# Values five tiles behind keys, the first maxima between the last value chunks, the last value group rounded on ScalarE

## The chip, the cores and the metric

One core of a Trainium2 chip runs the program; the other cores are idle. A time is device microseconds of one execution. TensorE (PE) multiplies matrices into PSUM, VectorE (DVE) and GpSimd (POOL) do element work and reductions, ScalarE (ACT) does activations and copies, SyncE (SP) issues most of the DMAs in the order in which they are written. Every engine works its own list in order and waits on semaphores.

## The reference

```python
x = x + tanh(g_xattn[0]) * xattn(layernorm(x), ctx_2048, Wq, bq, Wkv, bkv, Wp, bp)
x = x + tanh(g_ffn[0]) * moe(layernorm(x), Wg, W1, W3, W2, Ws1, Ws3, Ws2)
# xattn: 800 queries (8 x 100), 2888 keys (8 x 361), 16 heads of 32
q, k = fq_sym(q * scale, axis=-1), fq_sym(k, axis=-1)  # 8 bits, one step for a row and head
v = fq_sym(v, axis=2)                                  # one step for a column, over all 2888 keys
attn = fq_unsigned(softmax(q @ k.T))                   # 8 bits, one step for a row
out = (attn @ v) @ Wp + bp
```

The rounding of a value column needs the largest value over all keys: a value group must be complete before any of it is rounded. The mixture of experts behind the attention is not touched.

## The kernel before

Tokens stand in 7 tiles of 128 (the last has 32), keys in 23 tiles of 128, values in 4 groups of 128 columns (4 heads each), each group in 6 chunks of up to 512 keys: five of 512 and one of 328, 24 chunks in all.

**Projection loop.** For each key tile TensorE makes the key product (`project`, L549) and, from tile LEAD on, one value chunk (`make_values`, L575, line L586), both in fp32. A key tile goes through VectorE (read L1053, amplitude, rounding, multiplying back L1119), ScalarE (first of three bf16 parts, L911), GpSimd (rest, L1470), ScalarE (second part, L916) and GpSimd (third part, L1474), and SyncE stores it in DRAM (`key_parts`, L446). A product may start when VectorE has read the last but one; a value chunk when ScalarE has copied the last but one out of PSUM (`copy_values`, L899). VectorE bounds each copied chunk (`bound_values`, L1076) and after the sixth rounds the group to int16 and casts it to bf16 (`quantise_values`, L1083 to L1093); SyncE then transposes it (`transpose_values`, L438). With LEAD = 3, twenty chunks are in the loop and four behind it.

**Hand-over.** When all key tiles are stored and the last product is done, SyncE loads head 0's keys by four DMA transposes (`load_keys`, L427); head 1's follow when all value chunks are done, because their place overlays the context.

**Attention.** There are 100 tiles in a written order: for each of 16 heads six query tiles, and for each group of four heads one tile that holds the last 32 queries of the four. For each tile TensorE makes the scores twice, in four pieces for the maxima (`for_max`; VectorE reduces them, L1166) and in three for the exponentials (`for_exp`; ScalarE, L936, to 8-bit integers). VectorE turns the maxima into the bias of the exponentials (L1186). SyncE transposes the tile's probabilities (`transpose_p`, L472; two buffers), GpSimd widens them to bf16 (L1495), and TensorE multiplies them by the values (`weigh_values`, L645) four steps later. TensorE's order mixes these (`attention_step`, L657). SyncE's list interleaves the probabilities' transposes with key loads for later heads and, ahead of the second tile's probabilities, the transpose of the last value group. Four zero fills (L1135, L1137) on VectorE precede attention, and the last group's `quantise_values` stands in VectorE's list behind the second tile's maxima.

## Time and profile before

| | before |
|---|---|
| median of 3 runs | 1048.98 us (1046.87 to 1051.36) |
| profiled execution | 1048.64 us, of which the span is 1047.1 us |
| busy in the span | PE 94%, DVE 60%, ACT 49%, POOL 43% |
| chain that ended last, by engine | PE 52%, POOL 15%, DVE 11%, ACT 9%, issue 7%, DMA 5% |

The span runs from the first to the last instruction of the trace; the execution's own time lies 1.5 us above it. A row gives the start of an instruction, or of a run of like ones (x8), its length and what it does, and in brackets the time for which its engine had been idle and what released it. The projections of the keys and values lie between 50 and 208 us, attention between 208 and 597 us, the output projection and the mixture of experts behind.

### The profile page before, as it was taken

What the parts mean: (1) busy time and instruction counts of PE and PEld (TensorE: products, weight loads), DVE (VectorE), ACT (ScalarE), POOL (GpSimd) and SP (SyncE); (2) the same over time, 40 slices, a digit from 0 to 9 for tenths busy, and PEclk for the clock granted to TensorE, in tenths of its full rate; (3) what the DMA queues carried; (4) which work ended last, traced back from release to release, by engine and by line L of the source; (5) the groups of instructions that cost most, each with busy time, mean ns of one, the idle gap of its engine ahead of it and who ended that gap; (6) DMA issues with size and microseconds to landing.
All of it is one profiled execution on the core that took longest, in us unless ns stands there. A gap on an engine that the chain in (4) does not pass through costs nothing.

```text
span 1047.1 us, 16611 instructions
## 1 busy us (share of the span) xinstructions
PE 983.5 (94%) x5718; PEld 498.6 (48%) x5719; DVE 627.8 (60%) x1120; ACT 509.9 (49%) x1058; POOL 450.4 (43%) x319
## 2 busy tenths in 40 slices
PE   6999999879999999999999899999999999999993
PEld 3444444324334444444444457555656665666551
DVE  5686675499989999999999665811111111111156
ACT  2432223259999999999999822111211222121110
POOL 2053333227977777777677820371111111111165
PEclk9999999979999999999999998999999999999997
DMA  9974654678888888888776644144544654643155
GB/s 334 207 260 192 210 190 189 179 159 142 136 134 133 141 143 130 138 143 148 131 139 103 104 171 171 71 180 146 194 182 162 233 192 184 239 171 129 50 168 156
DMA packets 268272, 172.45 MB, mean 165 GB/s; under 512 B 239344, under 2 KB 239344, under 8 KB 265904
## 3 DMA queue, kind: packets, MB, share of 16 engines
q1 hardware_dynamic: 258512, 140.14, 54.7%
q0 software_dynamic: 9696, 31.47, 8.8%
q8 instruction: 39, 0.64, 0.3%
q14 instruction: 25, 0.20, 0.1%
HBM read 68.67 MB, written 44.63 MB: 108 GB/s over the span
## 4 chain that ended last, share of the span: by engine, by line
PE 52%; POOL 15%; DVE 11%; ACT 9%; issue 7%; DMA 5%; POOLq 0%; SPq 0%; DVEq 0%; ACTq 0%
PE ps L751 17%; POOL arena_a L1495 10%; PE ps L771 9%; ACT arena_a L936 7%; PE ps L603 6%; PE ps L586 6%; PE ps L563 6%; DVE span_max L1166 5%; POOL expert_in L1513 2%; PE ps L645 2%; PE ps L688 2%; DMA q_t<-parts 2%; PE ps L781 1%; PE ps L762 1%; POOL arena_b L1552 1%
## 5 line engine op out<-in xcount | busy, mean ns | idle before, releaser
L1166 DVE TENSOR_REDUCE span_max<-ps 128x1 f32<-128x481 f32 (+2 forms) x400 | 351.3, 904 | 21.0 <-PE ps L603 12.8
L936 ACT ACTIVATE arena_a<-ps,exp_bias,q_step 128x962 uint8<-128x962 f32 (+1 forms) x288 | 330.2, 1157 | 23.7 <-DVE exp_bias L1186 12.5
L1495 POOL CAST arena_a<-arena_a 128x3072 bf16<-128x3072 uint8 x100 | 274.3, 2752 | 123.3 <-DMA arena_a<-arena_a 113.8
L603 PE MATMUL ps<-arena_a,q_t 128*128 128x481 bf16 (+1 forms) x864 | 226.2, 376 | 20.0 <-DVE span_max L1166 8.0
L751 PE MATMUL ps<-arena_a,xt 128*128 x544 | 172.2, 459 | 1.8 <-issue 1.8
L1327 DVE TENSOR_TENSOR proj_d<-ps,proj_f 128x352 f32<-128x352 f32 x48 | 25.1, 524 | 200.5 <-ACT proj_f L984 200.5
L990 ACT COPY proj_r<-ps 128x128 f32<-128x128 f32 x144 | 28.4, 270 | 224.2 <-PE ps L762 224.2
L603 PEld LDWEIGHTS ps<-arena_a,q_t 128*128 128x128 bf16 x864 | 62.8, 98 | 150.9 <-ACT arena_a L936 69.5
L771 PE MATMUL ps<-arena_a,proj_r 128*128 (+3 forms) x288 | 133.5, 600 | 0.7 <-ACT proj_r L990 0.7
L751 PEld LDWEIGHTS ps<-arena_a,xt 128*128 128x128 f32 x544 | 100.4, 190 | 61.2 <-issue 17.9
L645 PEld LDWEIGHTS ps<-v_q,arena_a 128*128 128x128 bf16 x2400 | 75.5, 96 | 28.1 <-POOL arena_a L1495 9.8
L586 PE MATMUL ps<-arena_a 128*128 128x512 f32 (+1 forms) x192 | 83.0, 578 | 4.5 <-ACT xt L899 3.6
L563 PE MATMUL ps<-arena_a 128*128 128x512 f32 x184 | 82.6, 593 | 1.4 <-DVE proj_f L1053 1.1
L1519 POOL DMA_DIRECT2D xt<-expert_in x36 | 19.4, 539 | 147.8 <-PE ps L781 145.8
L645 PE MATMUL ps<-v_q,arena_a 128*128 128x32 bf16 (+1 forms) x2400 | 78.5, 178 | 2.8 <-POOL arena_a L1495 1.5
L603 PE MATMUL ps<-arena_b,q_t 128*128 128x481 bf16 (+1 forms) x288 | 75.0, 369 | 4.0 <-ACT arena_a L936 0.3
L771 PEld LDWEIGHTS ps<-arena_a,proj_r 128*128 128x128 f32 (+1 forms) x288 | 52.6, 192 | 50.4 <-issue 46.7
L751 PE MATMUL ps<-arena_a,q_t 128*128 128x352 f32 x224 | 73.2, 472 | 0.0
L1345 DVE COPY xt<-ps 128x512 f32<-128x512 f32 x34 | 23.5, 692 | 68.9 <-PE ps L771 68.9
L1523 POOL DMA_DIRECT2D expert_out<-xt x34 | 18.5, 544 | 106.5 <-DVE xt L1345 106.5
L984 ACT ACTIVATE proj_f<-ps 128x352 f32<-128x352 f32 x48 | 22.3, 464 | 83.5 <-PE ps L751 83.5
L586 PEld LDWEIGHTS ps<-arena_a 128*128 128x128 f32 x192 | 36.7, 193 | 49.2 <-issue 41.1
(167 smaller groups left out, 917.7 us busy)
## 6 DMA issues: line engine op xcount, KB each, us to landing
arena_a<-in_w_up SPq DMA_DIRECT2D x18, 1408.0 KB, 6.4
arena_a<-in_w_down SPq DMA_DIRECT2D x18, 768.0 KB, 8.4
key_parts<-parts SPq DMA_DIRECT2D x23, 512.0 KB, 2.7
expert_in<-xt SPq DMA_DIRECT2D x42, 256.0 KB, 3.0
xt<-expert_in POOLq DMA_DIRECT2D x36, 256.0 KB, 3.0
expert_out<-xt POOLq DMA_DIRECT2D x34, 256.0 KB, 2.3
arena_a<-in_ctx_t SPq DMA_DIRECT2D x3, 1536.0 KB, 13.2
expert_out<-xt SPq DMA_DIRECT2D x17, 256.0 KB, 3.1
```

The costliest lines, as they stand in the source:

```text
L563: last = mm(ps[:, 2 + j % 2, :], src, w_qkv[:, 0 if j < T else 1, k, :], start=(k == 0), stop=(k == DC - 1))
L586: last = mm(ps[:, 4 + v % 2, 0:w], w_qkv[:, 2, k, g * P:(g + 1) * P], ctx_sb[:, k, c * BANK:c * BANK + w], start=(k == 0), stop=(k == DC - 1))
L603: last = mm(ps[:, bank + b, 0:w], q_t[:, head, t * P:(t + 1) * P], k_t[head % NK][:, a:a + w], start=True, stop=True)
L645: last = mm(ps[:, OUT_BANK, 0:w], p_t[n % NPT][:, c, :], v_q[:, c, a:a + w], start=(c == 0), stop=(c == 2 * PC - 1))
L751: last = mm(ps[:, 1 + 2 * q + w, 0:INTER], src(k), arena_a[:, bass.ds(col + (w * DC + k) * INTER, INTER)], start=(k == 0), stop=(k == DC - 1))
L771: last = mm(ps[:, 6 + q, :], h_t[0:IW[c], q, c * P:(c + 1) * P], arena_a[0:IW[c], bass.ds(col + UPC + c * D, D)], start=(c == 0), stop=(c ...
L936: nc.scalar.activation(halves[:, :, a:a + w], ps[:, bank:bank + 2, 0:w], ACT.Exp, bias=exp_bias[:, n % 2:n % 2 + 1], scale=step_of, accum_ ...
L990: last = nc.scalar.copy(h_t[0:IW[c], q, c * P:(c + 1) * P], ps[0:IW[c], 5, c * P:(c + 1) * P])
L1166: v.tensor_reduce(span_max[:, n % 2, j:j + 1], ps[:, bank:bank + len(blocks), 0:w], AX.XY, ALU.max).then_inc(s_max, 1)
L1327: v.tensor_tensor(h_mul[:, q, 0:INTER], ps[:, 2 + 2 * q, 0:INTER], h_act[:, q, 0:INTER], ALU.mult).then_inc(s_hm, 1)
L1345: v.tensor_copy(y_rows[:, q, :], ps[:, 6 + (PRE + q) % 2, :]).then_inc(s_ya, 1)
L1495: p.tensor_copy(p_t[n % NPT].rearrange("p c q -> p (c q)").rearrange("p (j i) -> p j i", j=2), pt_u8[n % NT8].rearrange("p (i j) -> p j i" ...
```

## The change

LEAD becomes 5, so that 18 value chunks are in the loop. Three follow behind it; then TensorE makes the first tile's maxima, half of the second tile's, and the last three chunks between them (`FIRST_MAX` = 21 is the first of these). VectorE bounds these chunks between its first maxima. In the loop's last tile ScalarE copies a chunk ahead of its wait for the key tile; the tanh of the gates moves ahead of the last copies. The third group's `quantise_values` now stands behind the loop in VectorE's list, and its transpose behind the head-0 key loads in SyncE's. The last group's scale stays on VectorE; its rounding moves to ScalarE behind the first tile's exponentials, its cast to GpSimd, ahead of the first widening. The zero fills move from VectorE to GpSimd.

```diff
@@ -278,6 +278,7 @@
         s_vps = sem("value_product_done")
         s_vf = sem("values_copied")
         s_vmax = sem("value_maximum_done")
+        s_vscale = sem("last_value_scale_ready")
         s_vi = sem("value_integers_made")
         s_vb = sem("value_integers_ready")
         s_vq = sem("values_transposed")
@@ -346,7 +347,9 @@
         NV = (NKEY + BANK - 1) // BANK
 
 
-        LEAD = 3
+        LEAD = 5
+
+        FIRST_MAX = NG * NV - 3
 
         FIRST = 2
         NP = T + KT
@@ -591,7 +594,7 @@
                 project(T + kt)
                 if kt >= LEAD:
                     make_values(kt - LEAD)
-            for v in range(KT - LEAD, NG * NV):
+            for v in range(KT - LEAD, FIRST_MAX):
                 make_values(v)
 
             def products(n, blocks, bank):
@@ -648,9 +651,16 @@
 
             pe.wait_ge(s_qt[0], 16 * ((T + 1) // 2))
             pe.wait_ge(s_qt[1], 16 * (T // 2))
-            pe.wait_ge(s_vf, NG * NV)
             for_max(0, 0)
             for_max(0, 1)
+            make_values(FIRST_MAX)
+            for_max(0, 2)
+            for_max(0, 3)
+            make_values(FIRST_MAX + 1)
+            for_max(1, 0)
+            for_max(1, 1)
+            make_values(FIRST_MAX + 2)
+            pe.wait_ge(s_vf, NG * NV)
             for_exp(0, 0)
             for_exp(0, 1)
 
@@ -658,18 +668,25 @@
 
                 if n >= 2:
                     for_exp(n - 1, 0)
-                for_max(n, 2)
+                if n:
+                    for_max(n, 2)
                 if n >= 2:
                     for_exp(n - 1, 1)
-                for_max(n, 3)
+                if n:
+                    for_max(n, 3)
                 if n == 4:
                     pe.wait_ge(s_vq, 16 * (NG - 1))
                 if n == (NG - 1) * GT + 4:
                     pe.wait_ge(s_vq, 16 * NG)
                 weigh_values(n - 4)
-                for_max(n + 1, 0)
-                for_exp(n - 1, 2)
-                for_max(n + 1, 1)
+                if n == 1:
+                    for_exp(0, 2)
+                if n:
+                    for_max(n + 1, 0)
+                if n > 1:
+                    for_exp(n - 1, 2)
+                if n:
+                    for_max(n + 1, 1)
 
             def turn_attention(t):
 
@@ -903,6 +920,8 @@
             act.wait_ge(s_small, 16 * 7)
             for kt in range(KT):
                 j = T + kt
+                if kt == KT - 1:
+                    copy_values(kt - LEAD - 1)
                 act.wait_ge(s_kd, kt + 1)
                 if kt < 2:
                     act.wait_ge(s_qt[j % 2], 16 * ((T + 1 - j % 2) // 2))
@@ -911,14 +930,14 @@
                 nc.scalar.copy(parts[:, j % 2, :, 0, :], proj_d[:, j % 2, :].rearrange("p (h d) -> p h d", h=H)
                                ).then_inc(s_hi, 1)
                 if kt > LEAD:
-                    copy_values(kt - LEAD - 1)
+                    copy_values(kt - LEAD - (1 if kt < KT - 1 else 0))
                 act.wait_ge(s_rest, kt + 1)
                 nc.scalar.copy(parts[:, j % 2, :, 1, :], proj_r[:, j % 2, :].rearrange("p (h d) -> p h d", h=H)
                                ).then_inc(s_mid, 1)
-            for v in range(KT - LEAD - 1, NG * NV):
-                copy_values(v)
             act.wait_ge(s_small, 16 * 7)
             nc.scalar.activation(gates[:, :], gates[:, :], ACT.Tanh).then_inc(s_gate, 1)
+            for v in range(KT - LEAD, NG * NV):
+                copy_values(v)
 
             def exps(n):
 
@@ -951,8 +970,20 @@
 
             act.wait_ge(s_buf, NP8 + 1)
             act.wait_ge(s_tail, 16 * HG)
+
+            def round_last_values():
+
+                g = NG - 1
+                act.wait_ge(s_vscale, 1)
+                act.wait_ge(s_vq, 16 * g)
+                act.wait_ge(s_vi, g)
+                nc.scalar.activation(v_i[:, :, 0:PAIRS], v_fs[g % 2][:, 0:NKEY].rearrange("p (j i) -> p j i", j=2),
+                                     ACT.Identity, scale=v_inv[:, g:g + 1]).then_inc(s_vi, 1)
+
             for n in range(NTILE):
                 exps(n)
+                if n == 0:
+                    round_last_values()
                 if n == 3:
                     act.wait_ge(s_vi, NG)
                 if n >= 3:
@@ -1076,13 +1107,17 @@
                 v.tensor_reduce(v_part[:, c:c + 1], vals[:, c * BANK:c * BANK + w], AX.X, ALU.max,
                                 apply_absolute_value=True).then_inc(s_vmax, 1)
 
-            def quantise_values(g):
-
-                vals = v_fs[g % 2]
+            def scale_values(g):
+
                 dve.wait_ge(s_vmax, NV * (g + 1))
                 link(v.tensor_reduce(v_amax[:, g:g + 1], v_part[:, :], AX.X, ALU.max))
                 link(v.tensor_scalar(v_step[:, g:g + 1], v_amax[:, g:g + 1], 1.0 / 127.0, 1e-8, ALU.mult, ALU.max))
-                link(v.reciprocal(v_inv[:, g:g + 1], v_step[:, g:g + 1]))
+                return v.reciprocal(v_inv[:, g:g + 1], v_step[:, g:g + 1])
+
+            def quantise_values(g):
+
+                vals = v_fs[g % 2]
+                link(scale_values(g))
                 if g:
                     dve.wait_ge(s_vq, 16 * g)
                 else:
@@ -1124,23 +1159,13 @@
                     bound_values(v_)
                     if v_ % NV == NV - 1:
                         quantise_values(v_ // NV)
-            for v_ in range(KT - LEAD - 1, NG * NV):
+            dve.wait_ge(s_nq, T)
+            dve.wait_ge(s_tail, 16 * HG)
+            link(v.tensor_scalar(neg_tail_step[:, :], tail_step[:, :], -1.0, None, ALU.mult))
+            for v_ in range(KT - LEAD - 1, FIRST_MAX):
                 bound_values(v_)
                 if v_ % NV == NV - 1 and v_ // NV < NG - 1:
                     quantise_values(v_ // NV)
-
-
-            dve.wait_ge(s_vps, NG * NV)
-            for i in range(NP8):
-                v.memset(p_u8[i].bitcast(f32)[:, NKEY // 4:PPAD // 2], 0.0).then_inc(s_buf, 1)
-            dve.wait_ge(s_xz, 16 * len(ZEROED))
-            v.memset(attn[:, T - 1, :], 0.0).then_inc(s_buf, 1)
-
-            dve.wait_ge(s_buf, NP8 + 1)
-            dve.wait_ge(s_tail, 16 * HG)
-            link(v.tensor_scalar(neg_tail_step[:, :], tail_step[:, :], -1.0, None, ALU.mult))
-
-            dve.wait_ge(s_nq, T)
 
             def invert(inv, sums):
 
@@ -1171,6 +1196,8 @@
                 prev = n - 1
                 if n < NTILE:
                     maximum(n, 0)
+                if n == 1:
+                    bound_values(FIRST_MAX + 1)
                 if n:
                     dve.wait_ge(s_max, NM * n)
                     v.tensor_reduce(row_max[:, prev % 2:prev % 2 + 1], span_max[:, prev % 2, :], AX.X, ALU.max
@@ -1185,11 +1212,14 @@
                         dve.wait_ge(s_exp, NE * (prev - 1))
                     v.tensor_scalar(exp_bias[:, prev % 2:prev % 2 + 1], row_max[:, prev % 2:prev % 2 + 1],
                                     neg_step, LOG255, ALU.mult, ALU.add).then_inc(s_bias, 1)
+                if n == 0:
+                    bound_values(FIRST_MAX)
+                if n == 1:
+                    bound_values(FIRST_MAX + 2)
+                    scale_values(NG - 1).then_inc(s_vscale, 1)
                 if n < NTILE:
                     maximum(n, 2)
                     maximum(n, 3)
-                if n == 1:
-                    quantise_values(NG - 1)
                 for t in range(T - 1):
                     if n == COMPLETE[t] + INV_LAG:
                         invert_tile(t)
@@ -1475,6 +1505,15 @@
                                 ALU.subtract).then_inc(s_parts, 1)
 
 
+            pool.wait_ge(s_vps, NG * NV)
+            for i in range(NP8):
+                p.memset(p_u8[i].bitcast(f32)[:, NKEY // 4:PPAD // 2], 0.0).then_inc(s_buf, 1)
+            pool.wait_ge(s_xz, 16 * len(ZEROED))
+            p.memset(attn[:, T - 1, :], 0.0).then_inc(s_buf, 1)
+
+            pool.wait_ge(s_vi, NG)
+            p.tensor_copy(v_b.rearrange("p (j i) -> p j i", j=2)[:, :, 0:PAIRS], v_i[:, :, 0:PAIRS]).then_inc(s_vb, 1)
+
             def normalise(i, done, t):
 
                 pool.wait_ge(s_inv, i + 1)
```

## Rows read from the trace of the kernel before

**Rows 1.** Chain of waits in order of time: start us, length us, engine, output, line.
```profile
75.46 3.44 PE ps L563 x8
78.89 3.43 PE ps L586 x8
...
217.30 1.73 DVE arena_b L1091
```

**Rows 2.** Timeline, projection loop's end: start, us, engine, line, operation [idle before <-releaser].
```profile
178.78 3.60 PE L586 MATMUL ps<-arena_a 128*128 128x512 f32 x8
...
185.10 2.22 POOL L1474 TENSOR_TENSOR parts<-proj_r,parts 128x512 bf16<-128x512 f32 x1 [0.79 <-ACT parts L916]
...
185.65 3.60 PE L586 MATMUL ps<-arena_a 128*128 128x512 f32 x8
...
187.35 0.33 SPq L446 DMA_DIRECT2D key_parts<-parts  x1
...
188.02 0.68 DVE L1053 TENSOR_TENSOR proj_f<-ps,bias_rows 128x512 f32<-128x512 f32 x1
...
192.65 7.54 PE L586 MATMUL ps<-arena_a 128*128 128x512 f32 x13 [3.41 <-ACT xt L899]
...
195.28 0.34 SPq L446 DMA_DIRECT2D key_parts<-parts  x1
```

**Rows 3.** Timeline, start of attention.
```profile
197.94 14.92 SPq L427 DMA_TRANSPOSE arena_a<-key_parts  x8
...
207.95 1.58 PE L603 MATMUL ps<-arena_a,q_t 128*128 128x482 bf16 x7 [0.83 <-ACT xt L899]
...
208.44 0.48 DVE L1137 MEMSET xt<- 128x512 f32 x1
...
214.92 1.16 ACT L936 ACTIVATE arena_a<-ps,exp_bias,q_step 128x964 uint8<-128x964 f32 x1 [5.71 <-DVE exp_bias L1186]
...
221.09 6.74 PE L603 MATMUL ps<-arena_a,q_t 128*128 128x481 bf16 x17 [1.80 <-DVE span_max L1166]
...
221.82 1.16 ACT L936 ACTIVATE arena_a<-ps,exp_bias,q_step 128x964 uint8<-128x964 f32 x1 [2.45 <-DVE exp_bias L1186]
...
222.54 3.71 SPq L438 DMA_TRANSPOSE v_q<-arena_b  x1
...
226.43 1.44 SPq L472 DMA_TRANSPOSE arena_a<-arena_a  x1
...
230.61 2.75 POOL L1495 CAST arena_a<-arena_a 128x3072 bf16<-128x3072 uint8 x1 [4.50 <-DMA arena_a<-arena_a]
...
230.95 1.16 ACT L936 ACTIVATE arena_a<-ps,exp_bias,q_step 128x964 uint8<-128x964 f32 x1 [0.29 <-DVE exp_bias L1186]
...
234.62 1.16 ACT L936 ACTIVATE arena_a<-ps,exp_bias,q_step 128x964 uint8<-128x964 f32 x1
```

**Rows 4.** Stretches: length, then PE, PEld, DVE, ACT, POOL busy, PEclk, DMA, GB/s.
```profile
193.00:194.00 1.00, 1.00 (x2) 0.33 (x1) 0.32 (x1) 0.66 (x2) 0.31 (x1) 0.52 1.16 217
...
196.00:197.00 1.00, 1.00 (x3) 0.40 (x2) 0.00 (x0) 0.00 (x0) 0.00 (x0) 0.77 0.93 369
...
205.00:206.00 1.00, 1.00 (x5) 0.71 (x4) 0.33 (x1) 0.64 (x1) 0.00 (x0) 1.00 0.00 0
...
227.00:228.00 1.00, 0.83 (x4) 0.17 (x2) 0.83 (x1) 1.00 (x3) 0.00 (x0) 0.91 0.98 184
```

**Rows 5.** Timeline, early projection loop.
```profile
71.79 3.67 PE L586 MATMUL ps<-arena_a 128*128 128x512 f32 x8 [0.89 <-ACT arena_b L899]
```

**Rows 6.** Groups of 44 to 240 us: form, count, busy us, mean ns.
```profile
L899 ACT ACTIVATE xt<-ps,bv_col 128x512 f32<-128x512 f32 x10 | 6.8, 683 | 9.0 <-PE ps L586 9.0
...
L875 ACT CAST parts<-proj_i 128x2048 bf16<-128x2048 int16 x3 | 5.6, 1897 | 7.2 <-DMA q_t<-parts 7.2
```

**Rows 7.** Waits of SyncE's queue, 228 to 330 us: total, times, longest.
```profile
SPq L472 <- ACT arena_a L936: 29.8, 25, 2.3
...
SPq L471 <- POOL arena_a L1495: 24.6, 15, 2.8
```

## The prediction

> **What bounds the kernel now.** I read four views in this order: the page for the stages, the chain of waits for the place of the change, the timeline of its neighbourhood, and the waits of SyncE's queue for what comes after. The change sits where the key and value projections (to 208 us) hand over to attention (208 to some 597 us, 100 tiles).
>
> The projection loop is bound by TensorE: in the chain one key product or one full value chunk takes 3.43 us, and they follow each other without a gap [rows 1]. Ahead of the last key tile's reading that order breaks. VectorE rounds and casts the third value group inside the loop, so it reads the last key product, complete at 185.65 us, only at 188.02; that tile's parts are stored at 195.28, and TensorE, short of a value bank, idles 3.41 us until 192.65 [rows 2]. The head-0 key loads go out from 197.94 [rows 3], and the transfers are silent from 205 us on [rows 4], so I take 205.0 us for the keys' landing. TensorE does not feel it, since four value chunks keep it busy until 207.1; attention begins at 207.95 [rows 3].
>
> Then comes a ramp. The first exponentials start at 214.92, those of the second tile at 221.82, of the fourth at 230.95 and of the fifth at 234.62 [rows 3]. The step of 3.67 us between the last two is what the engines hold later; the 16.03 us from the first to the fourth are 5 us more than three such steps. In this ramp VectorE rounds and casts the last value group (the rounding alone 1.73 us, [rows 1]), and TensorE runs at half clock.
>
> **Part 1: keys earlier.** Two value chunks leave TensorE's queue ahead of the last key product: a short one (328 of 512 columns, 2.20 us of the 3.43) and a full one, 5.63 us together. In the early loop the stall of 0.89 us ahead of a value chunk goes [rows 5]; a shorter wait replaces it, because two more key products follow each other without a chunk between, and each needs VectorE's reading of the last but one. Net this is worth between 0 and 0.9 us; I take 0.2, so 5.8, and the last product is done at 179.85.
>
> VectorE now reads it at once. The tile before shows the time from product to store: 178.78 to 187.35, 8.57 us [rows 2]. This contains GpSimd's last subtraction at 2.22 us while VectorE rounds a group [rows 2], and I keep that: the third group's rounding moves behind the loop and meets the last tile's subtraction half a microsecond after it starts, as it did there. Without the collision it would be 1.1 us less. So the store is at 188.42 and the landing, at the old distance of 9.72 us from store to 205.0, at 198.1: 6.9 us earlier. TensorE's chunks behind the loop (2.20 and three of 3.43) end at 192.35, and it idles 5.7 us for the keys. This idling is the new wait; queued behind it are all maxima and the last three chunks.
>
> The third group's transpose moves in SyncE's queue behind the head-0 loads, its data being ready by then; nothing needs it before the fifth tile. The hyperbolic tangent with its table load moves ahead of copies that TensorE reaches later; I cost both at nothing.
>
> **Part 2: maxima between chunks.** From 198.1 TensorE has nine products of the maxima and chunks of 3.43, 3.43 and 2.20 us. Seven such products took 1.58 us [rows 3], so nine take 2.0 and all 11.0 us at full clock. It will not have that at once. After the idling at 189 to 192.65 the granted clock was 0.52 (1.2 GHz) at 193 us and full again from about 196.25, 3.6 us after work resumed [rows 4]; after a shorter gap it resumed at 221.09 at half clock, 0.40 us a product [rows 3], and was full from 227.1, 6.0 us later [rows 4]. Half the speed over 3.6 to 6.0 us loses 1.8 to 3.0 us; I take 2.4. The last chunk ends at 198.1 + 13.4 = 211.5.
> The Trainium skill, "TensorE: Matmul & The Clock Gate", section "HAM oscillation — how this bites in real kernels", warns of this form: a wait for a DMA lets the clock fall, and the work behind it starts cold. The trace agrees (0.52 after 3.41 us of idling). A sum without the rule would be 2.4 us better.
>
> Behind that chunk come the ScalarE copy, the two products for the exponentials and, on GpSimd, four zero fills that VectorE did before (the large one 0.48 us, [rows 3]); they run side by side, about 1.0 us. VectorE's maxima finish a microsecond before. First exponentials: 212.5, 2.4 us earlier than 214.92.
>
> **Part 3: the last group's rounding.** VectorE loses the rounding and the cast. ScalarE gains the rounding of 128x2888 behind its first tile. No row shows this on ScalarE; 512 elements cost 0.683 and 2048 cost 1.897 us [rows 6], which puts 2888 at 2.56; the bounds are 1.9 (as 2048) and 3.85 (at the 512 rate); I take 2.65. On ScalarE nothing hides it: the second tile's exponentials start at 212.5 + 3.5 + 2.65 = 218.65, against 221.82, 3.2 us earlier. For the third and fourth tiles TensorE will mostly be at half clock as before, since it waits on ScalarE during the rounding; between 3.67 us a tile (full clock) and the 4.56 measured I take 4.1. The fourth tile starts at 226.85, 4.1 us earlier (3.2 to 5.0).
>
> GpSimd gains the cast. The nearest row is its cast of 3072 bytes, 2.75 us [rows 3]; 2888 make 2.6, with bounds of 1.7 (VectorE's rounding of the same group, [rows 1]) and 5.5 (twice the row). It is ready at 218.65 + 2.6 = 221.2. The transpose of that group stands in SyncE's queue ahead of the second tile's probabilities, which left at 226.43 behind its 3.71 us [rows 3]. Now they leave at about 225.0: only 1.4 us earlier.
>
> **What is late next.** The probabilities' path (transpose, landing, widening on GpSimd, two buffers) takes over. The second tile's cast starts 4.18 us after its transpose issued (226.43 to 230.61, [rows 3]) and takes 2.75, so it ends at 231.9; the fourth tile's transpose waits for that. The third's follows a key load at about 228.3, its cast ends at 235.2 and frees the fifth. By that row of events the path is 1.4, 2.4, 2.6 and 2.9 us ahead of before, and TensorE's output product of the second tile, queued ahead of later maxima, holds the exponentials to about 3 us. Later SyncE's transposes wait 25 times on ScalarE (29.8 us) and 15 times on GpSimd's widening (24.6 us) between 228 and 330 us [rows 7], so both limits share that stretch: a lead of the exponentials over this path is not kept, and the path's own lead is. I take 3.2 us.
>
> **Sum.** The profiled execution took 1048.64 us, 1.5 more than its span of 1047.1 and 0.3 under the median of 1048.98. 1048.64 - 3.2 = 1045.4 us. Bounds: with the collision gone (1.1), the shorter half-clock stretch (0.6) and the fourth tile at 5.0 it would be 6.7 us, 1041.9; with the path's 1.4 alone 1047.2, and more with a slow cast.
>
> **Rivals.**
> 1. The whole lead is kept, 6.5 us: 1042.1. For it: SyncE waits more often on ScalarE than on GpSimd [rows 7]. Against: the second tile's late transpose, and the measured collision. 0.25.
> 2. The probabilities' path swallows the lead: GpSimd's cast near 5.5 us holds the group's transpose until 224.1 and the second tile's until 227.9, 1.5 us later than before; its later tiles recover some. I put the gain at 0.5 us: 1048.1. For it: one cast of GpSimd is all that the estimate rests on. Against: a same-sized one takes 2.75. 0.15.
> 3. Slower: TensorE's clock stays at half through all three chunks. They and the maxima take 22.0 instead of 11.0 us, the last chunk ends at 220.1, the first exponentials start at 221.1 and the second tile's at 227.2. With full clock then, the fourth tile starts at 234.6 against 230.95: 1052.3. It decides against the change at the first exponentials once the half clock lasts over 9.6 us (4.8 lost). Against: both stretches in [rows 4] end within 6.0 us. 0.05.
> 4. The keys do not come 6.9 us earlier, because VectorE and GpSimd, not TensorE, pace the loop; only the late reading goes (2.4, less the collision: 1.3). Keys at 203.7, second tile at 224.3, the second transpose some 4 us late: about 1052. Against: the two gapless steps of [rows 1], and no stall of the loop but that of [rows 5] and the last is long. 0.05.
>
> **How the numbers follow.** The forecast has 0.5, its own range 1043 to 1047.5. The range of 8 in 10 takes in rival 1 and most of rival 2: 1041.8 to 1048.9. A difference of 0.5%, 5.2 us, is about what this measurement can tell from none. Faster than 1043.7: most of rival 1 and a tail of the forecast, 0.28. Slower than 1054.2: only the far ends of rivals 3 and 4, 0.05. The same: 0.67.
>
> **What would show it.** The last key tile stored near 188.4; head-0 keys landed and the first maximum's product near 198; a TensorE gap of some 5 us before it and a granted clock near 0.5 in it; the first exponentials near 212.5 and the second tile's near 218.7; a ScalarE rounding of about 2.65 and a GpSimd cast of about 2.6 us; the second probability transpose near 225; attention's end some 3 us earlier. Wrong would be: no gap, full clock at once, a rounding or cast of twice the size, or a first maximum that is early while attention's end does not move.

## The result and the profile after

The changed kernel takes **1052.21 us**, the median of 20 runs (1047.02 to 1057.12); the kernel before, beside it, 1047.68 (1045.91 to 1051.36). The ratio is **1.0036, 95% interval 1.0023 to 1.0049**: some 4.5 us by the medians (3.8 by the ratio) or 0.4% slower, where 3.2 us less and a range of 1041.8 to 1048.9 were forecast. A few executions of the experiments below ran far slower at a lower clock throughout (one of 1232.64 us in e1, one of 1605.31 us in e3); the ratios leave them out. The profiled execution took 1051.55 us with a span of 1050.0, 2.9 above the span before. Of these, 2.3 lie in attention (the bias of its 99th tile starts at 591.82 against 589.48) and 0.6 behind it. A tile's bias is VectorE's last step ahead of its exponentials and serves here as the mark of when that tile comes.

From the page: busy time of each engine (share of the span, instructions), and the chain that ended last by engine.
```profile
PE 981.8 (94%) x5718; PEld 499.0 (48%) x5719; DVE 626.9 (60%) x1114; ACT 511.7 (49%) x1059; POOL 454.4 (43%) x324
...
PE 50%; POOL 20%; DVE 9%; issue 8%; ACT 6%; DMA 6%; SPq 1%; POOLq 0%; DVEq 0%; ACTq 0%
```
GpSimd, whose widening follows each probability transpose, holds 20% of the chain instead of 15, TensorE 50 instead of 52.

Timeline of the changed kernel at the hand-over (start, length, us; engine, line, operation; in brackets the idle time before and what ended it):
```profile
181.24 0.69 DVE L1084 TENSOR_TENSOR proj_f<-ps,bias_rows 128x512 f32<-128x512 f32 x1 [1.55 <-PE ps L566]
...
187.35 2.29 POOL L1504 TENSOR_TENSOR parts<-proj_r,parts 128x512 bf16<-128x512 f32 x1 [0.79 <-ACT parts L935]
...
199.67 1.36 PE L606 MATMUL ps<-arena_a,q_t 128*128 128x482 bf16 x3 [5.96 <-DMA arena_a<-key_parts]
...
200.83 5.95 PE L589 MATMUL ps<-arena_a 128*128 128x512 f32 x8
...
214.97 1.16 ACT L955 ACTIVATE arena_a<-ps,exp_bias,q_step 128x964 uint8<-128x964 f32 x1 [0.76 <-PE ps L606]
...
218.37 2.70 ACT L980 ACTIVATE arena_b<-xt,v_inv 128x2888 int16<-128x2888 f32 x1
...
220.96 1.16 ACT L955 ACTIVATE arena_a<-ps,exp_bias,q_step 128x964 uint8<-128x964 f32 x1
221.13 2.59 POOL L1515 CAST arena_b<-arena_b 128x2888 bf16<-128x2888 int16 x1 [6.70 <-ACT arena_b L980]
...
226.74 2.75 POOL L1534 CAST arena_a<-arena_a 128x3072 bf16<-128x3072 uint8 x1 [3.02 <-DMA arena_a<-arena_a]
...
228.20 1.16 ACT L955 ACTIVATE arena_a<-ps,exp_bias,q_step 128x964 uint8<-128x964 f32 x1 [0.29 <-DVE exp_bias L1213]
...
233.31 2.75 POOL L1534 CAST arena_a<-arena_a 128x3072 bf16<-128x3072 uint8 x1 [3.83 <-DMA arena_a<-arena_a]
...
236.12 0.81 PE L648 MATMUL ps<-v_q,arena_a 128*128 128x32 bf16 x24 [2.78 <-POOL arena_a L1534]
...
239.55 0.20 DVE L1213 TENSOR_SCALAR exp_bias<-row_max,neg_q_step 128x1 f32<-128x1 f32 x1
```
The reader is to see an early success and a late loss. The last key product is read as soon as it is done (181.24, before at 188.02, [rows 2]), and the first maxima start at 199.67 instead of 207.95 [rows 3], 8.3 us earlier. But TensorE has idled 5.96 us for the keys, three chunks still lie between it and attention, and the last of them ends at 213.65 (before: 207.1). So the first exponentials start at 214.97, where they were (214.92). The second tile's are 0.9 us ahead of before, the fourth's at 228.20 are 2.75 ahead. Then the lead is lost at one place: the product of the second tile's probabilities at 236.12 had to wait 2.78 us for GpSimd's widening of 233.31. Later maxima stand behind it, and the sixth tile's bias starts at 239.55, 7.00 us behind the fifth's instead of 3.75; before it stood at 238.13. Part of this step is the clock: TensorE came out of the wait of 2.78 us at half of it (row at 237 us below), where it was full before the change.

Why that widening is late is seen in SyncE's queue, in the same columns:
```profile
189.66 0.33 SPq L449 DMA_DIRECT2D key_parts<-parts  x1
...
192.33 5.19 SPq L430 DMA_TRANSPOSE arena_a<-key_parts  x4
197.57 3.73 SPq L441 DMA_TRANSPOSE v_q<-arena_b  x1
213.67 5.12 SPq L430 DMA_TRANSPOSE arena_a<-key_parts  x4
218.84 0.58 SPq L468 DMA_DIRECT2D arena_a<-in_wp  x1
219.46 3.29 SPq L475 DMA_TRANSPOSE arena_a<-arena_a  x1
222.79 2.48 SPq L430 DMA_TRANSPOSE arena_a<-key_parts  x1
225.32 3.75 SPq L441 DMA_TRANSPOSE v_q<-arena_b  x1
229.11 1.50 SPq L475 DMA_TRANSPOSE arena_a<-arena_a  x1
```
From 201.3 to 213.67 SyncE stands still. Next in its list is the wait for the last value chunk, ahead of head 1's keys, and behind these the load of the output weights (`in_wp`, 1 MB). Before, the chunk ended at 207.1; head 1's keys followed head 0's in one row of eight [rows 3], and the weights were issued at 212.91, 6.5 us ahead of the first tile's probabilities at 219.39, both by the trace of before. Now these leave at 219.46, 0.04 us behind the weights. Their issue takes 3.29 us (1.44 for the second tile's before, [rows 3]), their widening starts 7.28 us after it (226.74; 4.18 for the second tile's before, [rows 3]), a key row takes 2.48, the value group's transpose is pushed to 225.32, 1.6 us behind the end of its cast (221.13 + 2.59), and the second tile's probabilities, complete at 224.4, leave at 229.11. They left at 226.43 before.

The clock, in stretches (length; busy shares of PE, PEld, DVE, ACT, POOL; granted clock; DMA share, GB/s):
```profile
199.00:200.00 1.00, 0.33 (x1) 0.14 (x2) 0.00 (x0) 0.00 (x0) 0.00 (x0) 0.50 1.11 212
203.00:204.00 1.00, 1.00 (x2) 0.34 (x1) 0.00 (x0) 0.00 (x0) 0.00 (x0) 0.50 0.00 0
...
237.00:238.00 1.00, 1.00 (x4) 0.37 (x3) 0.23 (x1) 0.00 (x0) 1.00 (x1) 0.50 0.70 140
```
It fell to half in the wait for the keys (it was full until 198.7) and was full again by 205.6. The first chunk behind the keys took 5.95 us instead of the 3.60 of its like [rows 2].

### The profile page after: what moved, and what is told of

The parts are those of the page before. It is cut to its first block, busy times and chain, and to the rows that moved or that the text cites. A ratio compares the mean times of both kernels' runs of the same rounds, so it can differ in the third digit from the quotient of the medians.

```text
span 1050.0 us, 16610 instructions
## 1 busy us (share of the span) xinstructions
PE 981.8 (94%) x5718; PEld 499.0 (48%) x5719; DVE 626.9 (60%) x1114; ACT 511.7 (49%) x1059; POOL 454.4 (43%) x324
## 4 chain that ended last, share of the span: by engine, by line
PE 50%; POOL 20%; DVE 9%; issue 8%; ACT 6%; DMA 6%; SPq 1%; POOLq 0%; DVEq 0%; ACTq 0%
PE ps L768 18%; POOL arena_a L1534 15%; PE ps L788 9%; PE ps L589 5%; PE ps L606 5%; PE ps L566 4%; ACT arena_a L955 4%; POOL expert_in L1552 2%; DVE span_max L1191 2%; DMA q_t<-parts 2%; PE ps L705 2%; PE ps L648 2%; PE ps L798 1%; PE ps L779 1%; DMA arena_b<-expert_out,slot_i 1%
## 5 line engine op out<-in xcount | busy, mean ns | idle before, releaser
L606 PE MATMUL ps<-arena_a,q_t 128*128 128x481 bf16 (+1 forms) x864 | 223.2, 372 | 22.9 <-DMA arena_a<-key_parts 6.0
L1021 ACT COPY proj_r<-ps 128x128 f32<-128x128 f32 x144 | 28.4, 270 | 224.1 <-PE ps L779 224.1
```

The source lines that it names most:

```text
L606: last = mm(ps[:, bank + b, 0:w], q_t[:, head, t * P:(t + 1) * P], k_t[head % NK][:, a:a + w], start=True, stop=True)
L1021: last = nc.scalar.copy(h_t[0:IW[c], q, c * P:(c + 1) * P], ps[0:IW[c], 5, c * P:(c + 1) * P])
```

## Experiments

Times are medians beside runs of the kernel before (1047.5 to 1047.8 in each of three series); in brackets stand the ratio to it and its 95% interval. Three theories are named in the expectations. **Q**: SyncE's queue, filled late because the last chunk is late, delays the second tile's probabilities. **C**: the last chunks run behind a wait at half clock. **R**: ScalarE's rounding of the last group delays the second tile.

**Output weights later (e1), last group's transpose later (e2), both (e3, shown).**
```diff
             load_keys(1)
-            sp.dma_start(wp_sb, wp.rearrange("(k p) n -> p k n", p=P)).then_inc(s_wp, 16)
...
-                if n == 2:
-                    transpose_values(NG - 1)
                 if n >= 1:
                     transpose_p(n - 1)
+                if n == 5:
+                    transpose_values(NG - 1)
+                if n == 6:
+                    sp.dma_start(wp_sb, wp.rearrange("(k p) n -> p k n", p=P)).then_inc(s_wp, 16)
```


> The changed kernel, with the load of the output weights (1 MB, SyncE) moved from ahead of the first tile's probabilities to behind the sixth's. Theory Q (SyncE's queue: the last value chunk now ends at 213.65 instead of 207.1 us, so head 1's keys, the output weights and the last value group's transpose stand ahead of the second tile's probabilities, which leave at 229.1 instead of 226.4): they leave near 227.5, the sixth tile's bias moves from 239.55 to about 238, median about 1.5 us below the changed kernel's 1052.2. Theory C (the clock: the lead is lost because TensorE makes the last three chunks cold after its wait for the keys): no change, 1052. Theory R (ScalarE's rounding of 2.7 us is the loss): no change, 1052.

> The changed kernel, with the last value group's transpose moved in SyncE's list from ahead of the second tile's probabilities to behind the fifth's. Theory Q: the second tile's probabilities leave near 225.3 instead of 229.1, the sixth tile's bias comes near 236.5, median about 3 us below 1052.2, 1049. Theory C and theory R: no change, 1052.

> Both moves at once. Theory Q: the second tile's probabilities leave near 224.4, as soon as its exponentials are done; the fourth tile's lead of 2.75 us on the kernel before is kept to the end of attention, median about 1048, 4 us below the changed kernel and about as the kernel before or 1 below. Theory C and theory R: no change, 1052.


Measured: e1 1050.31 (1.0021, 1.0001 to 1.0042), e2 1050.63 (1.0014, 0.9994 to 1.0034), e3 1051.99 (1.0034, 1.0016 to 1.0052). Q had expected 1050.7, 1049 and 1048. In the ramp all do what Q says: the second tile's probabilities leave at 227.74, 223.71 and 223.58, and in e2 and e3 the long step is gone, the sixth tile's bias being at 234.68 and 234.46 (after: 239.55). The medians hardly follow; e3 is as slow as the changed kernel. In e2 and e3 the 99th tile's bias does come earlier (587.30 and 589.06, after: 591.82), and what their profiled executions lose again lies behind attention (last section), so for e2, whose interval holds both the time before and that after, nothing is settled. e3's queue shows why (columns as above):
```profile
236.00 4.75 SPq L441 DMA_TRANSPOSE v_q<-arena_b  x1
...
242.34 0.90 SPq L484 DMA_DIRECT2D arena_a<-in_wp  x1
243.35 2.50 SPq L474 DMA_TRANSPOSE arena_a<-arena_a  x1
245.89 3.25 SPq L430 DMA_TRANSPOSE arena_a<-key_parts  x1
```
The moved transfers stand in front of later tiles. The value transpose takes 4.75 us there, a probability transpose behind the weights 2.50, and from the ninth tile to the eleventh 10.94 us pass (245.49 to 256.43) instead of 7.35. In e1 the weights, issued at 244.02, do it too: the key row behind them takes 2.76 instead of 1.6. A transfer put later in a full queue moved the loss of e1 and part of that of e3.

**One of the three chunks ahead of the maxima (e4, shown; VectorE's bounds follow), and all three (u2).** In u2 `FIRST_MAX` is `NG * NV`, the three `make_values` between the maxima go, and VectorE bounds their chunks behind the loop.
```diff
-        FIRST_MAX = NG * NV - 3
+        FIRST_MAX = NG * NV - 2
...
             for_max(1, 1)
-            make_values(FIRST_MAX + 2)
```


> The changed kernel with chunk 21 ahead of the first maxima (two instead of three chunks between maxima), so that TensorE works in most of its wait for the keys. Theory C: the wait falls from 6.0 to 2.5 us, the last chunk ends near 209 instead of 213.65, first exponentials near 210 instead of 214.97, median 1048. Theory Q: the same start of head 1's keys, 4.5 us earlier, also brings the second tile's probabilities to about 225: 1048 too, so this run sizes the part and does not tell Q from C; runs without a change of TensorE's order do that. Theory R: the rounding stays, 1051 to 1052.

> The changed kernel without its second part: all 24 value chunks ahead of the first maxima; the rounding on ScalarE, the cast on GpSimd and LEAD = 5 stay. Theory C: TensorE does not wait 6 us for the keys and stays at full clock, the last chunk ends near 203, the maxima start near 203.5 (199.67 in the changed kernel) but the first exponentials near 210 instead of 214.97, and the median is about 1046.5, as with one chunk ahead of the maxima (1046.6). Theory Q: head 1's keys start 10 us earlier, at 203, so SyncE is clear before the first tile's probabilities: 1046 to 1047 too. Theory R: the rounding stays: 1051 to 1052.


Measured: e4 1046.56 (0.9987, 0.9967 to 1.0006); u2 **1043.9 (0.9971, 0.9960 to 0.9983)**, 8.3 us under the changed kernel (6.8 by the ratios) and below the one before. u2's timeline and its queue:
```profile
181.36 21.74 PE L589 MATMUL ps<-arena_a 128*128 128x328 f32 x56
...
202.94 0.77 PE L606 MATMUL ps<-arena_a,q_t 128*128 128x482 bf16 x3
```
```profile
203.13 5.28 SPq L430 DMA_TRANSPOSE arena_a<-key_parts  x4
208.45 0.58 SPq L468 DMA_DIRECT2D arena_a<-in_wp  x1
213.41 1.48 SPq L475 DMA_TRANSPOSE arena_a<-arena_a  x1
...
222.36 1.50 SPq L475 DMA_TRANSPOSE arena_a<-arena_a  x1
```
All the chunks run without a gap from 181.36, and TensorE never waits for the keys. Its first maxima come 3.3 us later than in the changed kernel, yet the last chunk ends at 203.1 instead of 213.65. With it SyncE's wait ends at 203.13, the weights are issued 5 us ahead of the first probabilities, whose issue takes 1.48 us, and the second tile's leave at 222.36, 6.8 us earlier. The interleaving, taken by itself, is what costs. In e4 the weights still stand right ahead of the first probabilities (issued at 211.84; the probabilities' issue takes 4.03 us), but the value group's transpose leaves 1.0 us after its cast instead of 1.6, 6.4 us earlier than in the changed kernel, and the kernel is no slower than before. So the load beside the first probabilities does not make the kernel slower wherever it stands there; in the changed kernel it meets a queue that is already late.

**The weights ahead of the wait (e5), and the same in the kernel before (q1).**
```diff
+            sp.dma_start(wp_sb, wp.rearrange("(k p) n -> p k n", p=P)).then_inc(s_wp, 16)
             sp.wait_ge(s_vps, NG * NV)
             load_keys(1)
-            sp.dma_start(wp_sb, wp.rearrange("(k p) n -> p k n", p=P)).then_inc(s_wp, 16)
```


> The changed kernel, with the load of the output weights moved in SyncE's list to just before its wait for the last value chunk, where the transfers are silent (203 to 214 us in the changed kernel), so that it is paid nowhere else. Theory Q (SyncE's queue is where the lead is lost): the first tile's probabilities leave near 218.4 with a transpose of 1.5 instead of 3.3 us, the second tile's near 227 instead of 229.1, the sixth tile's bias near 237.5 instead of 239.55, median 1050. Theory C (the cold last chunks between the maxima): no change, 1052. Theory R (ScalarE's rounding): no change, 1052.

> Control: the kernel before, with the load of the output weights moved ahead of SyncE's wait for the last value chunk, as in the run where that move took 4.4 us off the changed kernel. Theory Q (the load costs only where it stands in the first probabilities' way): in the kernel before SyncE is done with it at 213.5 and its bytes have moved by 218 us, ahead of the first probabilities at 219.4, so the move is worth nothing here: 1047.6, within 0.7. Rival (the load is in the way in any order): 1045 or less.


Measured: e5 **1047.76 (1.0004, 0.9989 to 1.0019)**, 4.4 us under the changed kernel, with intervals that do not meet and the 99th tile's bias at 587.81, 4.0 earlier; q1 1047.37 (1.0002, 0.9985 to 1.0018), nothing. e5's queue:
```profile
201.89 0.58 SPq L466 DMA_DIRECT2D arena_a<-in_wp  x1
212.45 5.12 SPq L430 DMA_TRANSPOSE arena_a<-key_parts  x4
217.62 1.84 SPq L475 DMA_TRANSPOSE arena_a<-arena_a  x1
...
222.53 3.63 SPq L441 DMA_TRANSPOSE v_q<-arena_b  x1
226.21 1.57 SPq L475 DMA_TRANSPOSE arena_a<-arena_a  x1
```
and from its timeline the cast of the last value group:
```profile
219.91 2.59 POOL L1515 CAST arena_b<-arena_b 128x2888 bf16<-128x2888 int16 x1 [6.70 <-ACT arena_b L980]
```
The weights move while SyncE stands at its wait. The first probabilities issue in 1.84 us, the second tile's leave 2.9 us earlier. By the medians nearly the whole loss of 4.5 us goes with this one line. It belongs to the change, since in the kernel before the same move is worth nothing.

How the line gives it back is seen only in part. In e5's profile the half clock ended at 202.9 instead of 205.6, so that the first tile's bias was 1.2 us ahead of the changed kernel's. Executions alone do as much: e2 and e3 have the changed kernel's code up to there, and their first bias stands at 212.35 and 212.65 (after: 213.57, e5: 212.34). Without these 1.2 us the second tile's probabilities leave 1.7 us earlier, the sixth tile's bias comes 1.3 us and the 99th's 2.8 us earlier; e1, counted in the same way, has 1.6 and 1.8 us at the first two. So the ramp shows less than half of the 4.4 us; where the rest arises was not traced.

A long step is left in e5 (6.6 us at the sixth tile). The second tile's probabilities stand behind the value group's transpose, and this now leaves at 222.53, 0.03 us after GpSimd's cast has ended (219.91 + 2.59); in e1, u2 and w1 it is the same 0.03 us. With the weights out of the way, the rounding on ScalarE and the cast behind it are therefore the next limit: e5's second tile leaves at 226.21, about as before the change (226.43).

**LEAD = 5 alone in the kernel before (p1).**
```diff
-        LEAD = 3
+        LEAD = 5
```


> The kernel before with LEAD = 5 alone: all value chunks ahead of the maxima, last group rounded and cast on VectorE. The last product is done near 181 instead of 185.65 us and is read at once, and TensorE's stall of 3.41 us ahead of a chunk may go. All theories: attention starts near 203.5 to 204.5 instead of 207.95, and since nothing is moved into SyncE's or ScalarE's way, the median is 3 us below the kernel before, about 1044.5. If the last chunks stall for ScalarE's copies, which here has no copy ahead of its wait in the last tile, 1046 to 1047.


Measured 1048.51 (1.0003, 0.9986 to 1.0020), not the 1044.5 to 1047 that were expected. The last key tile is stored at 189.17, 6.1 us earlier, but:
```profile
186.54 21.34 PE L586 MATMUL ps<-arena_a 128*128 128x512 f32 x48 [2.48 <-ACT arena_b L899]
208.70 1.58 PE L603 MATMUL ps<-arena_a,q_t 128*128 128x482 bf16 x7 [0.83 <-ACT xt L899]
```
Six chunks now stand behind the loop, TensorE idles 2.48 us once, in front of them, for a copy of ScalarE's (the change's edit that puts this copy ahead of the wait for the key tile is missing here), and the maxima start at 208.70 (207.95 before). Early keys are worth nothing here while TensorE has chunks to do.

**The rounding cut away (r0).** ScalarE rounds 8 of the 2888 columns of a row; the rest of the last value group is left out, so later stages get other data, and only the ramp is read (its total, 1076.56, is not comparable).
```diff
-                nc.scalar.activation(v_i[:, :, 0:PAIRS], ...
+                nc.scalar.activation(v_i[:, :, 0:4], ...
```


> The changed kernel with ScalarE's rounding of the last value group cut to 8 of 2888 elements of each row (the rest of that group is left out of the computation, GpSimd's cast and the transpose stay). Theory R: ScalarE starts the second tile's exponentials 2.5 us earlier and the median falls by about 2.5 us to 1049.7. Theory Q: SyncE reaches the group's transpose at 225.3 only, after its data were ready in any case (223.7), so the second tile's probabilities leave at 229 as before and the sixth tile's bias stays near 239.5: 1052. Theory C: 1052.


```profile
218.21 0.30 ACT L980 ACTIVATE arena_b<-xt,v_inv 128x8 int16<-128x8 f32 x1
...
219.31 4.19 SPq L475 DMA_TRANSPOSE arena_a<-arena_a  x1
219.32 1.16 ACT L955 ACTIVATE arena_a<-ps,exp_bias,q_step 128x964 uint8<-128x964 f32 x1 [0.81 <-DVE exp_bias L1213]
...
229.92 1.50 SPq L475 DMA_TRANSPOSE arena_a<-arena_a  x1
```
The rounding takes 0.30 us instead of 2.70 and the second tile's exponentials start 1.6 us earlier, at 219.32. Still the second probabilities leave at 229.92 and the sixth tile's bias is at 240.12. So R does not set this ramp as long as the weights stand in it: the queue, whose first probability transpose took 4.19 us here, ends later. That the rounding is the next limit behind the queue is seen in e5.

**TensorE kept busy in the wait (w1, upon e5).**
```diff
+            for i in range(12):
+                mm(ps[:, 6, :], w_qkv[:, 2, i % DC, 0:P], ctx_sb[:, i % DC, 0:BANK], start=True, stop=True)
             pe.wait_ge(s_qt[0], 16 * ((T + 1) // 2))
```


> The changed kernel with the output weights loaded early (1047.8 without the rest of this edit) and with twelve products whose result nobody reads in TensorE's wait for the head-0 keys, so that it does not idle. Theory C: the clock stays at full, chunk 21 takes 3.4 instead of 4.4 to 5.7 us, the first exponentials start about 2 to 3 us earlier (near 211) and the median is 2 to 3 us lower, about 1045.3. Rival (the chunks between the maxima are not on the path, or the probabilities' path holds everything): 1047.8. If the added products delay the first maxima by as much as they save, also 1047.8, and the trace shows it.


Measured 1049.24 (1.0018, 1.0001 to 1.0035), 1.5 us above e5, with intervals that meet.
```profile
192.68 10.46 PE L653 MATMUL ps<-arena_a 128*128 128x512 f32 x24
202.98 0.77 PE L606 MATMUL ps<-arena_a,q_t 128*128 128x482 bf16 x3
203.59 3.60 PE L589 MATMUL ps<-arena_a 128*128 128x512 f32 x8
```
The twelve products took 10.46 us, more than the wait of 5.96 us that they were to fill, and ended at 202.98; head 0's key loads were issued at 191.47, and by the 7.2 us from issue to landing in the changed kernel (192.33 to 199.54 in its chain) the keys had, by this estimate, been there since 198.7. The clock stayed full and the first chunk took 3.60 us instead of 5.95; the last ended at 214.06 (after: 213.65). The added work ate what it saved. C's 2.4 us for that chunk are measured, its worth in time by itself is not: no shorter filling was tried.

**All causes taken away (b1):** u2 and e5 together, the last group rounded ahead of the first exponentials, its transpose right behind head 1's keys.
```diff
+            sp.dma_start(wp_sb, wp.rearrange("(k p) n -> p k n", p=P)).then_inc(s_wp, 16)
             sp.wait_ge(s_vps, NG * NV)
             load_keys(1)
-            sp.dma_start(wp_sb, wp.rearrange("(k p) n -> p k n", p=P)).then_inc(s_wp, 16)
+            transpose_values(NG - 1)
...
+            round_last_values()
             for n in range(NTILE):
                 exps(n)
-                if n == 0:
-                    round_last_values()
```


> A version from what the runs point to: LEAD = 5, all value chunks ahead of the maxima (1043.9 alone), output weights loaded ahead of SyncE's wait, the last group's scale right behind its last chunk's maximum, its rounding on ScalarE ahead of the first exponentials, where ScalarE waits some 6 us for the first bias, and its transpose behind head 1's key loads. If the rounding (2.7 us of ScalarE) and the transpose ahead of the second tile's probabilities (3.7 us of SyncE) are on the path in the changed kernel: second exponentials near 214, no long step between the fourth and the sixth tile, attention's end near 580, median about 1040.5. If only the weights and the cold chunks matter: 1043 to 1044.


Measured **1040.53 (0.9931, 0.9905 to 0.9957)**: 7.0 us below the kernel before, 11.7 below the changed one, in six runs.
```profile
204.56 2.70 ACT L976 ACTIVATE arena_b<-xt,v_inv 128x2888 int16<-128x2888 f32 x1 [1.84 <-DMA v_q<-arena_b]
...
207.32 2.59 POOL L1504 CAST arena_b<-arena_b 128x2888 bf16<-128x2888 int16 x1 [4.39 <-ACT arena_b L976]
...
209.74 1.16 ACT L951 ACTIVATE arena_a<-ps,exp_bias,q_step 128x964 uint8<-128x964 f32 x1 [2.48 <-PE ps L605]
...
214.02 1.16 ACT L951 ACTIVATE arena_a<-ps,exp_bias,q_step 128x964 uint8<-128x964 f32 x1 [0.76 <-DVE exp_bias L1207]
```
```profile
209.94 3.70 SPq L441 DMA_TRANSPOSE v_q<-arena_b  x1
213.69 1.52 SPq L476 DMA_TRANSPOSE arena_a<-arena_a  x1
```
ScalarE, idle between its last copy and the first exponentials, rounds there at no cost. The group's transpose is through before any probabilities wait, the second tile's leave at 217.56, the second to sixth tile's biases follow 3.67 to 3.74 us apart, and the 99th tile's bias starts at 579.84, 9.6 us ahead of before. The 3.4 us below u2 belong to the weights' and the rounding's places together; these were not run apart upon u2.

## Why the prediction was wrong

**What held.** The late reading went (181.24). The collision of GpSimd's last subtraction with VectorE's rounding came as costed: 2.29 us (2.22 before, [rows 2]) against 1.16 of the tile before it. (The Trainium skill, "SBUF — State Buffer", section "Who interferes with whom", has VectorE, in its two-port modes, and GpSimd share a pair of ports that one of them holds for a whole instruction; the trace agrees to within 0.15 us: the subtraction lasts about as long as VectorE's rounding has left, 1.27 us, and its own 1.16; VectorE's cast behind it took 1.75, its own 0.91, as alone in the trace of before, and the 0.98 that the subtraction had left.) Store to landing, TensorE's wait of 5.7 (5.96), the clock at half in it and for 5.9 us behind it (3.6 to 6.0), the rounding of 2.65 (2.70) and the cast of 2.6 (2.59) are within their bounds. The tanh with its table load (187.22) and the zero fills on GpSimd (213.70 to 214.44, beside ScalarE's copy) cost nothing, as assumed.

**What was mis-sized.** Early keys: 5.8 us were taken for the two chunks less a small stall, 4.6 came (the last product done at 181.04, not 179.85). The stall of 0.89 [rows 5] did not go; the loop has stalls of 0.41 and 1.20 us there. The first maxima came 1.6 us later than the forecast, the half clock cost 2.9 instead of 2.4 (2.35 in the chunk, 0.58 in its three maxima), and the last chunk ended at 213.65, not 211.5. So the first exponentials had no lead where 2.4 us were expected, and the rounding and the cast, which hang on them, came 2.5 us late: the cast ended at 223.72, not 221.2. This alone still left the exponentials of the second and fourth tiles 0.9 and 2.75 us ahead.

Two readings of the clock were off. By [rows 4] it was full from 196.46, not 196.25 (0.77 over 196 to 197 us is half the clock for 0.46 us). And the stretch that ended near 227.1 had not lasted 6.0 us: in the trace of before the clock was at half from 213.5 on, 13.7 us in all, with TensorE at work in most of them. That row did not speak against rival 3 as the prediction says.

**The step that failed** is the second probability transpose, which Part 3 lets leave "at about 225.0" and on which "What is late next" builds. It left at 229.11. Of the 4.1 us, 2.5 are the late cast just named, a mis-sized start. The other 1.6 are a wait in SyncE's queue that the prediction does not have: the group's transpose, ready at 223.72, left at 225.32. The prediction took the order of SyncE's queue from the trace of before, the value group's transpose ahead of the second tile's probabilities, and moved only that. It did not carry the later end of the last chunk, 211.5 in its own sum against 207.1, into the one wait of SyncE on it. Behind this wait stand head 1's keys (5.12 us) and the weights, and behind them every probability. By its own 211.5 the weights would have been issued at 216.7 and the first probabilities, complete at some 216, right behind them: the collision could have been read off. The price it could not have: none of its rows had a probability transpose beside a load. By the medians of e5 this queue is worth nearly all of the loss; but with it cleared the kernel is only where it was before, which leaves the forecast gain of 3.2 us to the late start and to the rounding and cast that hang on it. u2, which removes the late start, and b1, which takes the rounding off the path as well, are 3.7 and 7.0 us below the kernel before.

**The rivals.** Rival 4's figure (about 1052, a second transpose some 4 us late) gives the time that came, by luck: the keys were early, and the second transpose left 2.7 us after that of before. Rival 3 needed a half clock of over 9.6 us; it lasted 6.8 in all. Rival 2 has the right place, the probabilities' path, and nearly the right moment (a cast that ends at 224.1), but the wrong cause: the cast took 2.59 us and started late.

Of the 4.5 us of the medians the two profiled executions show 2.9; the rest is not traced, and single executions of the same code differ by as much (below).

## What to carry to other kernels

Work that is moved later on one engine moves every wait on its end: list who waits on that semaphore and what stands behind each such wait, on the DMA-issuing queue first. Filling an engine's wait with work that must be done anyway pays only if nothing else waits for that work; here three chunks put behind the keys held up 1 MB and a whole queue of transposes, and doing them first was 8.3 us better. A load that nobody needs soon belongs where its queue stands still (e5), and a rounding where its engine idles (b1, there together with the load).

## What was unexpected of the hardware

A plain 1 MB load issued just ahead of a transpose from SBUF to SBUF slowed the transposes behind it: 3.29 us of issue instead of 1.44 and 7.28 us to the widening instead of 4.18; in e2, r0 and e4, with the same order, the issues are 3.23, 4.19 and 4.03, and in e1, without the load, 1.52.

Stretches of half clock do not lie at the same places in each execution. At the hand-over of the kernel before, TensorE idled 3.41 us [rows 2] and went on at 1.2 GHz (0.52 at 193 us, [rows 4]). In q1, whose code is the same up to there, it idled 3.42 us and went on at full clock (columns as above):
```profile
193.00:194.00 1.00, 1.00 (x4) 0.44 (x3) 0.00 (x1) 0.97 (x2) 0.21 (x1) 1.00 1.16 217
```
q1's first maxima start 2.0 us earlier (205.94) and its 99th tile's bias stands 2.6 us earlier (586.86), yet the medians of the two agree within 0.2 us. So the prediction's row was one outcome of two, and against q1 the changed kernel's attention ends 5.0 us later, not 2.3.

Behind attention every profiled kernel has a stretch of half clock between 626 and 646 us, and e2, e3 and e4 have another between 709 and 720 us. e2 there (columns as above; TensorE had idled 1.75 us ahead, as long as in the kernels before and after, where it went on at full clock):
```profile
714.00:715.00 1.00, 1.00 (x3) 0.67 (x2) 0.00 (x0) 0.00 (x0) 0.00 (x0) 0.50 0.20 78
```
One such group of eight products took 5.06 us there and 2.63 before. From the 99th tile's bias to the end of the span it is 457.6 us before, 458.2 after, 455.9 in e5, but 462.2 in e2 and 461.2 in e3, whose code is the same there. A single profile's span, or its end of attention, therefore can't settle differences of some microseconds; medians of many runs can.
